# ScalarE copies the query projection after the duo's second exponential instead of before it

## The reference, cut to what matters

```python
xn = layernorm(x)                                  # x: 16 x 1024 x 256, f32
q = relu(xn @ Wq.T + bq)                           # 16 heads of 16 columns
k = relu(keys @ Wk.T + bk); v = relu(values @ Wv.T + bv)   # 1024 rows, shared by the batches
attn = softmax(q_h @ k_h.T / sqrt(16))             # per batch and head: 1024 x 1024
a = (attn @ v_h), heads put back, transposed as the reference does
y = clip((xn @ sign(Wf).T) * scale + bias, -100, 100)
out = x + (a + xn) + y
```

## Time and profile before

| | |
|---|---|
| median of three runs | 2841.65 us |
| time of the profiled execution | 2842.26 us |
| its span, first to last instruction | 2840.4 us |
| mean granted TensorE clock | 0.985 of full speed |
| busy: TensorE (PE), ScalarE (ACT), VectorE (DVE), GpSimd (POOL) | 97%, 86%, 82%, 33% |

### The profile page before, as it was taken

The page is one execution under the profiler, slowest core; times in us unless marked ns, Lnnn a source line. Parts: engine busy times, 40 slices in busy tenths (PEclk is TensorE's granted clock), DMA queues, the critical chain, the costliest instruction groups (busy, mean ns, idle before and its releaser), DMA issues.

```text
span 2840.4 us, 61159 instructions
## 1 busy us (share of the span) xinstructions
PE 2766.6 (97%) x17860; PEld 1147.5 (40%) x17860; DVE 2337.9 (82%) x4578; ACT 2449.8 (86%) x2949; POOL 938.4 (33%) x845
## 2 busy tenths in 40 slices
PE   8899999999999999999999999999999999999996
PEld 4434344443434434444443444334444443444331
DVE  6788888888888888888888888888888888888940
ACT  4788988888888888888898888888888888888996
POOL 4304334241343314334242343314333242343001
PEclk8699999999999999999999999999999999999998
DMA  7111221121221121121121221121121121221111
GB/s 143 60 40 57 66 68 46 50 66 57 63 70 52 40 70 55 65 70 33 59 70 55 65 66 51 44 70 55 65 66 34 62 69 55 65 64 36 48 55 38
DMA packets 78636, 167.74 MB, mean 59 GB/s; under 512 B 28547, under 2 KB 32646, under 8 KB 76326
## 3 DMA queue, kind: packets, MB, share of 16 engines
q1 hardware_dynamic: 78374, 164.19, 19.2%
HBM read 36.71 MB, written 17.83 MB: 19 GB/s over the span
## 4 chain that ended last, share of the span: by engine, by line
PE 75%; issue 10%; DVE 5%; ACT 2%; POOL 1%; DVEq 0%; POOLq 0%; ACTq 0%
PE value_ps L611 29%; PE ring L633 27%; PE score_ps L597 13%; DVE mx L962 4%; ACT probs L809 2%; PE score_ps L677 1%; PE score_ps L662 1%; PE score_ps L679 1%; PE score_ps L666 1%; PE score_ps L664 1%; POOL fin L1100 1%; DVE excess L937 0%; PE ring L642 0%; DVE mx L937 0%; DVE sums L994 0%
## 5 line engine op out<-in xcount | busy, mean ns | idle before, releaser
L809 ACT ACTIVATE probs<-score_ps 128x1024 f32<-128x1024 f32 x2048 | 1992.4, 1024 | 228.4 <-PE score_ps L597 222.0
L962 DVE TENSOR_REDUCE mx<-ring 128x1 f32<-128x512 f32 x2952 | 1900.5, 684 | 239.6 <-PE ring L633 214.7
L633 PE MATMUL ring<-kstack,qstack 48*128 48x512 f32 x3444 | 1169.2, 468 | 16.1 <-DVE mx L962 3.7
L611 PE MATMUL value_ps<-probs,vones 128*32 128x512 f32 x8192 | 1091.6, 605 | 1.3 <-ACT taken L816 0.5
L633 PEld LDWEIGHTS ring<-kstack,qstack 48*128 48x128 f32 x3444 | 489.8, 183 | 1073.4 <-DVE mx L962 1037.9
L597 PE MATMUL score_ps<-qstack,kstack 51*128 51x512 f32 x4096 | 813.8, 415 | 9.6 <-ACT probs L809 4.7
L937 DVE CUSTOM_DVE_ANT_0 excess<-ring,excess 128x512 f32<-128x512 f32 x512 | 353.1, 690 | 137.4 <-PE ring L633 120.3
L1100 POOL TENSOR_TENSOR dense<-dense,affine 128x512 f32<-128x512 f32 x128 | 164.3, 1284 | 860.1 <-ACT dense L859 858.6
L597 PEld LDWEIGHTS score_ps<-qstack,kstack 51*128 51x128 f32 x4096 | 394.2, 186 | 122.7 <-ACT probs L809 61.3
L825 ACT ACTIVATE excess<-ring 128x512 f32<-128x512 f32 x492 | 293.6, 597 | 1.2 <-PE ring L633 0.9
L611 PEld LDWEIGHTS value_ps<-probs,vones 128*32 128x32 f32 x8192 | 161.4, 108 | 321.4 <-issue 289.5
(11 more groups left out here) (93 smaller groups left out, 1413.4 us busy)
## 6 DMA issues: line engine op xcount, KB each, us to landing
qstack<-parts SPq DMA_DIRECT2D x768, 64.0 KB, 2.5
fin<-taken SPq DMA_DIRECT2D x256, 128.0 KB, 2.9
xin<-x SPq DMA_DIRECT2D x16, 1024.0 KB, 5.2
base_cur<-base_new SPq DMA_DIRECT2D x16, 1024.0 KB, 5.5
fin<-recip SPq DMA_DIRECT2D x32, 512.0 KB
out<-fin SPq DMA_DIRECT2D x32, 512.0 KB, 2.6
qstack<-proj SPq DMA_DIRECT2D x256, 12.0 KB
kstack<-base_cur SPq DMA_DIRECT2D x16, 128.0 KB, 6.0
```

The costliest lines, as they stand in the source:

```text
L611: mm = pe.matmul(value_ps[h4 * 32:(h4 + 1) * 32, :], vones[:, 2 * tp + c, hh * HALF + side * PAIRS + 2 * g + j, :, :], probs[:, q % 2 * GR ...
L633: pe.matmul(ps[:, :], qstack[nh][rows, pair, st * P:(st + 1) * P], keys, start=True, stop=True).then_inc(s_mm, 1)
L809: nc.scalar.activation(probs[:, q % 2 * GROUP + u % GROUP, :], score_ps[src][:, :], ACT.Exp, scale=EXP_SCALE).then_inc(s_probs, 1)
L962: nc.vector.tensor_reduce(most, src[:, :], AX.X, ALU.max).then_inc(s_mx, 1)
```

## The change

```diff
                     job = duo_job(hh, some, d)
                     if att:
                         exponentials(*att, 2 * d, at["first"])
-                    if "between" in at:
+                    if "between" in at and job[0] == "turn":
                         take_job(b, hh, *job, at["between"])
                     if att:
                         exponentials(*att, 2 * d + 1, at["second"])
+
+                    if "between" in at and job[0] == "project":
+                        take_job(b, hh, *job, at["between"])
                     if "behind" in at:
                         take_job(b, hh, *job, at["behind"])
```

## The result

The changed kernel takes 2855.54 us (median of five runs, 2854.15 to 2857.59) against 2841.65 us: ratio 1.005, 95% interval 1.0038 to 1.0061. It is slower by 13.9 us, where 13.6 us and 2855.2 us were forecast. The profiled execution has a span of 2854.9 us.

What follows compares the result with a forecast made beforehand. TensorE, chained with VectorE's reductions, was taken to bound the kernel; 9.0 + 4.3 + 0.3 = 13.6 us on 2841.65 gave 2855.2 us (+0.48%), own range 2851.3 to 2861.4, 8 in 10 range 2848 to 2863.

Steps and rivals of the forecast that it cites:

- The earlier exponential is worth nothing: Second exponential of a projection's duo starts 0.15 us sooner, but its readers come later, so no gain.
- 0.43 us late, 0.30 lost: Next unit's scores after each moved copy: weight load 0.43 us late, scores end 0.30 us later.
- The credit of 0.13 for the restart: At the late scores load: load and matmul starting together end 0.50 us after the load, against 0.63 when prefetched.
- 30 x 0.30 behind duos 9 and 13: Pairs without a job behind these duos take each 0.30 us delay whole: 9.0 us.
- 16 x 0.27 behind duo 11 and the first duo 7: 15 delays behind duo 11 plus duo 7 of the first half-step, without reciprocals, 0.27 us each: 4.3 us.
- the slack of 0.03 at tile 3: Behind duo 11, tile 3's matmul absorbs 0.03 us of the 0.30 delay, leaving 0.27.
- The reciprocals swallow 14 stalls: Behind duo 7 in the other 14, tile 3's load waits for VectorE's reciprocals anyway: 0 to 0.1 each, taken as 0.3 us.
- The sign that I gave for it: Duo 7 to duo 9 grows by almost nothing where there are reciprocals, by 0.3 us in the first half-step.
- GpSimd: Its split after the second copy of `hh` = 0 has to wait some 0.6 us for the later copy, at no cost.
- The fourth rival: Each of 60 stalls drops TensorE to 1.2 GHz for the pair of duos behind it: 3136 us, chance 0.01.
- One sign was wrong: Scores' loads newly wait about 0.4 us for the projection's copy, 60 times, 0.2 to 0.3 also idle for matmuls.
- The two other signs of being wrong: VectorE's idle time before the joining reduction shrinks by TensorE's loss, or ScalarE's exponentials no longer wait for scores.

Runs made afterwards that it cites:

- the quarter copy: The changed kernel with each moved copy taking only the first 128 of 512 columns: 2842.3 us, ratio 0.9999 to the kernel before.
- the copy in four: The changed kernel with each moved copy cut into four of 128 columns, the last one signalling: 2885.31 us, ratio 1.0151 to the kernel before.

## Why the prediction was right, point by point

- **TensorE's chain bounds the kernel, so ScalarE's idle time has no price.** Right. 39.1 us of ScalarE's idle time were filled and the kernel got slower.
- **The earlier exponential is worth nothing.** Right, by the quarter copy: same order, 0.0 us. It starts 0.04 behind its scores, as said, and the copy 0.93 behind it.
- **0.43 us late, 0.30 lost.** Right: 0.44 late and 0.30 lost in the timeline; 0.62 to 0.64 for the longer turn copies, forecast 0.61 to 0.64. The credit of 0.13 for the restart is real: without it the pairs of the table would have grown by 0.43.
- **30 x 0.30 behind duos 9 and 13.** Behind duo 13 the pair 12 to 14 grew by 0.27 and the next by 0.01; in `hh` = 1 with the reciprocals away, duo 8 to 10 grew by 0.27. The terms are about 0.28 rather than 0.30.
- **16 x 0.27 behind duo 11 and the first duo 7.** 0.29 to 0.31 each, so little of the slack of 0.03 at tile 3 shows. The errors of these two terms, about -0.6 and +0.4 us, cancel for the most part; that is luck.
- **The reciprocals swallow 14 stalls.** Right, shown by moving them: 13.1 us with them in place, 17.1 without. The sign that I gave for it has to be read with care: from the first exponential of duo 7 to that of duo 9 it is 6.32 us before and 6.63 after, since the swallowing comes behind the latter, at tile 3; from second exponential to second exponential it is 6.73 and 6.71.
- **GpSimd.** It waits, as said, but not for 0.6 us: 14.9 us in 15 times, so 0.99 on average and 1.17 in this batch (the row below, timeline of 1430 to 1450 us). The stall behind duo 11 delays the second copy, but not GpSimd, and I left it out there. The rest is GpSimd itself, whose additions ahead of the splits start up to 0.5 us earlier or later from batch to batch in both kernels, as their data land (before, in this batch, they waited 0.28 us for a DMA). It costs nothing; the pair 14 to 16 is the same to 0.01 us.

```profile
1443.60 1.04 POOL L1103 TENSOR_TENSOR parts<-proj,const 128x512 fp32r<-128x512 f32 x1 [1.17 <-ACT proj L853]
```

- **The clock.** It stays at 2.4 GHz through the stalls: granted 1.00 from 400 to 2640 us, and the profile's line of the clock shows tenths of 9 throughout but for the start and the end. In the copy in four, whose stalls are 0.75 us long, the granted clock between 400 and 2600 us is 1.00 too. The fourth rival had priced a fall at 60 x 4.9 = 294 us. By the micro-idle rule of the Trainium skill ("TensorE: Matmul & The Clock Gate", "A second HAM failure mode: psum-queue depth-cycling") the clock could have fallen and risen again; the runs here don't agree with it.
- **One sign was wrong.** I wrote that the matmuls too would show 0.2 to 0.3 us of idle time, and that the prediction would be wrong if only the loads did. Only the loads do, and it is right: a matmul that starts together with its load is drawn 0.50 us long instead of 0.40, and the one before it to its modelled end, so the profile books nearly all of the stall as busy time of TensorE: 14.7 us over the whole span, and in the inner stretch 12.5 of the 13.1 us (union of its matmuls' records). Where the stall is longer it does show: in the copy in four the matmuls sat idle for 29.8 us in 58 times. The two other signs of being wrong stayed away: VectorE's wait for the tile that it joins is 110.4 us in 333 times where it was 110.0 in 330, and the exponentials wait more for scores than before, 228.8 us against 181.5 between 400 and 2600 us.

The total fits to 0.3 us by the medians. Some of that is luck, as the late rise of the clock alone moves single executions by 2 us; the inner stretch says 13.1 where 13.6 was forecast.

## What to carry to other kernels

Idle time in front of an instruction isn't a reason to move it: ask which semaphore it raises, who takes the buffer next, and how long it is from the copy's end to that user's weight load. Where two PSUM tiles go in strict turn, the copy that frees the tile of the next unit belongs ahead of the exponential that nobody waits for yet; moving it behind delays its end by the exponential's step and by the wait for that exponential's own scores (here 0.92 + 0.43 = 1.35 us), and costs that less the time that the tile lay free (0.92), less what the restart gives back (0.13), and less what a later wait on another engine swallows. Such a swallowing wait (here 0.54 us of reciprocals put where VectorE had no room) is itself worth removing, 4.6 to 6.3 us here: put side work on the engine that is second in the chain ahead of a long job of the first.

## What the runs showed that I had not expected

- A stall of the matmul engine can appear as busy time: +14.7 us busy at a span of +14.5 us, while its idle time hardly moved (27.2 us before and 27.9 after in the inner stretch).
- A copy that starts right behind another activation lasts 0.682 us instead of 0.688.
- The moment at which TensorE's clock rises at the start varies between profiled executions that do the same work up to there. Of eleven such kernels (the one with the moved turn copies left out) five ran 121 to 128 us at a granted 0.98 to 1.00 and six at 0.59 to 0.69, and the second cost about 2 us. For effects of a few microseconds the distance between two instructions behind that point is a sharper measure than the run's time.
